# Attention's tail and the front of the first expert layer in another order, on one core

## The chip, the core and the metric

One core of a Trainium2 chip runs the whole program. Its engines work through lists of their own, in order: PE is TensorE (matmuls), DVE is VectorE, ACT is ScalarE, POOL is GpSimd, and SP issues transfers. They wait for each other by counting semaphores alone. The metric is the device time of one execution in microseconds (us); lower is better.

## What is computed

Two blocks in a row work on x, 16 sequences of 128 tokens (2048 tokens, width 256). Cut to what matters here:

```python
x = x + tanh(g_xattn[0]) * attention(layernorm(x), ctx)   # 16 heads of 16, quantised q, k, v and weights; softmax over all 2048 keys; then @ Wp + bp
x = x + tanh(g_ffn[0]) * moe(layernorm(x))                # rms norm, router to 32 experts (best 4 per token), a shared expert (704 wide) scaled by a sigmoid
x = x + tanh(g_xattn[1]) * wkv(layernorm(x), ctx)
x = x + tanh(g_ffn[1]) * moe2(layernorm(x))               # 8 experts, best 2, a shared expert
```

The change touches the end of the first line and the start of the second: the projection `@ Wp`, the norm of the new rows, the router, each token's choice of experts, and the shared expert's hidden layer.

## The kernel before, in words

**Attention.** 256 heads (16 tiles of 128 queries, 16 heads each) are worked through one after the other. A head is two units of 1024 keys (`fill_unit`, 512 units, numbered 0 to 511): two matmuls fill one of two pairs of PSUM banks, ScalarE takes the exponentials to bytes (line 485), SP transposes the head's bytes by DMA, GpSimd widens them to bf16 (the cast of line 537, into one of three buffers), and TensorE sums the values in 16 small matmuls a head (`sum_values`, line 252). A unit waits for the exponentials of the unit two before it. A cast waits until the head three before it has its values. VectorE takes maxima all along (line 426) until 701; its last tile is finished by `finish_tile`, which frees the outputs (`s_ofree`).

**The tail.** The tiles are taken in four groups of four. A group's attention outputs are turned (`turn_outputs`, line 262, 8 transposes), copied to SBUF (`copy_outputs`), and projected in two halves (`project_half`, line 270, 8 float32 matmuls each, written here as 4 instructions with two records each in the trace). VectorE adds each half to x (`add_projection`, line 369) and takes the group's statistics (`group_statistics`); ScalarE works out the deviations (`deviations`), and the group's rows are normalised: for group 0 by VectorE (`normalise`), for the others by ScalarE (`normalise_rows`, line 1358).

**The front.** Per group: the rows are turned (`turn_rows`, line 281) and copied (`copy_rows`), multiplied with the router (`router`, line 292), the logits copied (`copy_logits`), and VectorE then goes through `choose` (the four best experts; ends with `choices_marked`), `take_slots`, `weigh` (ends with `destinations_ready`, on which SP stores the rows and loads experts' weights) and `mark_slots` (a 2048-wide comparison, line 1472). TensorE counts places between them (`places`, lines 1285 and 1288) and fills a table (`fill_table`, line 1298), for which GpSimd multiplies numbers in (lines 1275 and 1276). Beside it the shared expert's hidden layer is worked out for group 0 in six columns c (`hidden0` in the code): TensorE's gate product (line 1166) and up product (line 1174), ScalarE's Silu (line 1197), VectorE's product of the two (line 1207). There is one PSUM bank for the gate and one for the up product, so that the gate of column c waits for Silu c-1, and the up product of column c for VectorE's product c-1:

```python
pe.wait_ge(sm_["gates_passed"], n)     # in shared_gate_tensor
...
pe.wait_ge(sm_["hidden_ready"], n)     # in shared_up_tensor
```

The front ends when the table is taken and the shared answers of group 0 (line 1187, 12 us of matmuls) are under way; the 32 experts follow them on TensorE.

**Order.** Nothing schedules: each engine's order is the order in which `attention_*` and `front_*` are written out by hand. Silu needs another table of ScalarE's than Ln and Exp, so each change between them loads one (`ACT_TABLE_LOAD`).

## Time and profile before

| | us |
|---|---|
| median of 3 runs | 1172.74 (1171.52 to 1173.14) |
| span of the profiled execution | 1171.5 |
| TensorE busy | 1066.6 (91%) |
| VectorE busy | 956.1 (82%) |
| ScalarE busy | 892.2 (76%) |
| GpSimd busy | 702.5 (60%) |

The profile gives the profiled execution's span and no time of its own beside it; the median lies 1.24 us above that span, and what is said of the difference between the two kernels is added to the median. All times in the stages below are us from the span's start. The attention's units end at about 724, the front reaches from there to about 778, the first group's shared answers to 791, and the experts start behind them.

### The profile page before, as it was taken

What the parts mean: (1) busy time and instruction counts of PE and PEld (TensorE: products, weight loads), DVE (VectorE), ACT (ScalarE), POOL (GpSimd) and SP (SyncE); (2) the same over time, 40 slices, a digit from 0 to 9 for tenths busy, and PEclk for the clock granted to TensorE, in tenths of its full rate; (3) what the DMA queues carried; (4) which work ended last, traced back from release to release, by engine and by line L of the source; (5) the groups of instructions that cost most, each with busy time, mean ns of one, the idle gap of its engine ahead of it and who ended that gap; (6) DMA issues with size and microseconds to landing.
All of it is one profiled execution on the core that took longest, in us unless ns stands there. A gap on an engine that the chain in (4) does not pass through costs nothing.

```text
span 1171.5 us, 24138 instructions
## 1 busy us (share of the span) xinstructions
PE 1066.6 (91%) x8396; PEld 608.8 (52%) x8396; DVE 956.1 (82%) x1748; ACT 892.2 (76%) x1546; POOL 702.5 (60%) x626
## 2 busy tenths in 40 slices
PE   8988898889988988898889988999999999999995
PEld 5743444444444444444444447756654455557774
DVE  6999999999999999999999996853328888843335
ACT  4779999999999999999999996635534567734440
POOL 3016888888787878787878785457641001543331
PEclk9999999999999999999999999799999999999998
DMA  6797987888788888888776664867937003433326
GB/s 192 121 163 146 171 171 162 171 171 173 161 171 171 173 164 173 173 169 164 155 118 110 112 109 65 244 182 213 316 98 300 1 0 85 138 102 101 102 89 222
DMA packets 388928, 176.36 MB, mean 151 GB/s; under 512 B 330542, under 2 KB 373779, under 8 KB 388809
## 3 DMA queue, kind: packets, MB, share of 16 engines
q1 hardware_dynamic: 382104, 157.85, 62.2%
q0 software_dynamic: 6480, 16.77, 4.2%
q8 instruction: 69, 1.13, 0.4%
q14 instruction: 51, 0.41, 0.1%
q10 hardware_dynamic: 224, 0.20, 0.1%
HBM read 52.70 MB, written 43.59 MB: 82 GB/s over the span
## 4 chain that ended last, share of the span: by engine, by line
PE 51%; DVE 33%; ACT 5%; issue 5%; DMA 3%; POOL 2%; SPq 1%; POOLq 0%; ACTq 0%; DVEq 0%
DVE top L426 26%; PE bank L234 10%; PE bank L220 9%; PE bank L1187 4%; PE bank L2599 4%; PE bank L252 4%; PE bank L1580 3%; PE bank L2615 3%; PE bank L1174 2%; PE bank L1166 2%; ACT weight L485 2%; PE bank L270 1%; PE bank L1598 1%; PE bank L682 1%; POOL dispatched_rows L1823 1%
## 5 line engine op out<-in xcount | busy, mean ns | idle before, releaser
L485 ACT ACTIVATE weight<-bank,bias,sq_all 128x1024 uint8<-128x1024 f32 x512 | 610.2, 1201 | 24.1 <-PE bank L234 18.9
L426 DVE TENSOR_REDUCE top<-bank 128x1 f32<-128x512 f32 (+1 forms) x683 | 610.1, 951 | 11.9 <-PE bank L220 1.6
L537 POOL CAST weight<-turned 128x2048 bf16<-128x2048 uint8 x256 | 479.4, 1895 | 44.8 <-PE bank L252 23.2
L234 PE MATMUL bank<-kT,query 128*128 128x512 bf16 x1024 | 307.7, 382 | 11.8 <-ACT weight L485 4.8
L252 PEld LDWEIGHTS bank<-v_sb,weight 128*128 128x128 bf16 x4096 | 172.0, 97 | 103.4 <-POOL weight L537 1.9
L220 PE MATMUL bank<-kT,qspace 64*128 64x512 bf16 x687 | 134.9, 386 | 55.0 <-DVE top L426 55.0
L252 PE MATMUL bank<-v_sb,weight 128*128 128x16 bf16 x4096 | 172.5, 170 | 0.6 <-POOL weight L537 0.6
L220 PE MATMUL bank<-kT,query 128*128 128x512 bf16 x337 | 127.8, 379 | 1.6 <-DVE top L426 1.4
L234 PEld LDWEIGHTS bank<-kT,query 128*128 128x128 bf16 x1024 | 59.8, 96 | 103.8 <-ACT weight L485 61.8
L1823 POOL DMA_INDIRECT dispatched_rows<-qspace,put x32 | 37.1, 1161 | 117.8 <-DVE qspace L2376 108.6
L485 ACT ACTIVATION_READ_ACCUMULATOR weight<-bank,bias,sq_all 128x1 f32 x512 | 101.3, 198 | 0.0
L220 PEld LDWEIGHTS bank<-kT,qspace 64*128 64x128 bf16 x687 | 33.3, 92 | 91.7 <-DVE top L426 86.5
L2738 POOL DMA_INDIRECT answered_rows<-yrow,target x39 | 38.0, 974 | 68.1 <-ACT yrow L2665 62.6
L2697 DVE TENSOR_TENSOR eh<-esil,bank 128x176 f32<-128x176 f32 x39 | 13.2, 338 | 60.8 <-ACT esil L2658 60.8
L520 POOL TENSOR_TENSOR shift<-shift,nsq_all 128x4 f32<-128x4 f32 (+1 forms) x65 | 13.0, 201 | 82.5 <-DVE shift L430 82.4
L220 PEld LDWEIGHTS bank<-kT,query 128*128 128x128 bf16 x337 | 32.6, 97 | 54.1 <-DVE top L426 35.4
L2599 PE MATMUL bank<-late,erowT 128*128 x156 | 52.6, 460 | 0.0
L1187 PE MATMUL bank<-sw,hT 128*128 128x256 f32 x192 | 47.5, 392 | 0.5 <-DVE source L1479 0.5
L1166 PE MATMUL bank<-xT,sw 128*128 128x512 f32 (+1 forms) x96 | 46.2, 604 | 1.6 <-ACT sil L1197 1.6
L1674 DVE TENSOR_TENSOR qspace<-wp,bank 128x176 f32<-128x176 f32 x32 | 10.8, 338 | 45.1 <-ACT wp L1631 45.1
L1174 PE MATMUL bank<-xT,sw 128*128 128x512 f32 (+1 forms) x96 | 45.8, 599 | 1.1 <-DVE hT L1207 1.1
L1713 POOL DMA_INDIRECT answered_rows<-yrow,target x32 | 31.9, 997 | 19.7 <-ACT yrow L1638 13.3
(350 smaller groups left out, 1466.2 us busy)
## 6 DMA issues: line engine op xcount, KB each, us to landing
dispatched_rows<-zeros SPq DMA_DIRECT2D x32, 524.0 KB, 3.2
...
turned<-weight SPq DMA_TRANSPOSE x256, 3.1
```

What stands on the lines that cost most here:

```text
L220: pe.matmul(bank[:, k, :], q, kT[rows, h // 2, kb * 512:(kb + 1) * 512], start=True, stop=True).then_inc(s_blk, 1)
L234: mm = pe.matmul(unit[u % 2][:, v * 512:(v + 1) * 512], query2[:, t % 2, h, :], kT[:, h // 2, first + v * 512:first + (v + 1) * 512], star ...
L252: mm = pe.matmul(bank[:, 7, h * HD:(h + 1) * HD], weight[:, m % 3, r // 2, :, r % 2], v_sb[:, r, h * HD:(h + 1) * HD], start=(r == 0), sto ...
L426: ve.tensor_reduce(top[:, first:first + count], bank[:, first % 3:first % 3 + count, :], AX.X, ALU.max).then_inc(s_max, 1)
L485: ac.activation(weight8[:, n % BYTES, u * 1024:(u + 1) * 1024], unit[u], ACT.Exp, bias=bias[:, n:n + 1], scale=sq_all[:, n:n + 1], accum_o ...
L537: po.tensor_copy(weight[:, n % 3, :, :, :].rearrange("p c q two -> p (c q two)"), turned8[:, n % 3, :, :].rearrange("p c q -> p (c q)").bi ...
L1166: mm = pe.matmul(bank[0:w, 0, :], swg[:, k, c * P:c * P + w], xT[:, k, g * 512:(g + 1) * 512], start=k == 0, stop=k == CK - 1)
L1174: mm = pe.matmul(bank[0:w, 1, :], swu[:, k, c * P:c * P + w], xT[:, k, g * 512:(g + 1) * 512], start=k == 0, stop=k == CK - 1)
L1187: mm = pe.matmul(bank[:, 6 + k % 2, 0:C], hT[0:w, c, k * P:(k + 1) * P], swd[0:w, c, :], start=c == 0, stop=c == NW0 - 1)
L1823: po.indirect_dma_start(out=dispatched1, out_offset=bass.IndirectOffsetOnAxis(ap=put1[:, t, k:k + 1], axis=0), in_=rows0[:, t, 0:ROW1], in ...
L2599: mm = pe.matmul(bank[:, 2 + b % 2, 0:2 * F1], erowT1[:, b % 2, k, :], w1gu[:, expert[b], k, :], start=k == 0, stop=k == CK - 1)
L2738: po.indirect_dma_start(out=answered1, out_offset=bass.IndirectOffsetOnAxis(ap=target1[:, b:b + 1], axis=0), in_=yrow1[:, b % YRING, :], i ...
```

## The change

Of the six half projections of groups 0 to 2, two now stand ahead of the attention's last unit and four behind it (five and one before). `finish_tile` for the last tile moves from VectorE's front to its tail, ahead of all of `choose`; group 3's outputs are turned, copied and projected ahead of the first `choose` and `places`. ScalarE's deviations of group 0 move from before the last head's exponentials to behind them. The rest of the front is in a new order on TensorE, ScalarE and VectorE. No instruction but one table load is added or taken away: ScalarE loads a table three times in the front instead of five.

```diff
--- before.py
+++ after.py
@@ -313,6 +313,10 @@
                     u = fill_unit(pe, u)
                     step = sum_values(pe, step, 9, u)
 
+                def values_to(head):
+                    nonlocal step
+                    step = sum_values(pe, step, NT * head - step, u)
+
                 unit_and_values()
                 unit_and_values()
                 pe.wait_ge(s_max, NRED)
@@ -321,35 +325,30 @@
                 unit_and_values()
                 pe.wait_ge(sm_["outputs_copied"], 1)
                 turn_outputs(pe, 1, 0)
+                unit_and_values()
+                unit_and_values()
                 project_half(pe, 0, 0, 2)
+                unit_and_values()
                 unit_and_values()
                 unit_and_values()
                 pe.wait_ge(sm_["projections_added"], 1)
                 project_half(pe, 0, 1, 2)
+                while u < NUNIT:
+                    unit_and_values()
                 pe.wait_ge(sm_["outputs_copied"], 2)
                 turn_outputs(pe, 2, 0)
-                unit_and_values()
-                unit_and_values()
+                values_to(NHEAD - 3)
                 pe.wait_ge(sm_["projections_added"], 2)
                 project_half(pe, 1, 0, 2)
-                unit_and_values()
+                values_to(NHEAD - 2)
+                pe.wait_ge(s_exp, NUNIT)
+                project_half(pe, 1, 1, 3)
+                values_to(NHEAD)
                 pe.wait_ge(sm_["projections_added"], 3)
-                project_half(pe, 1, 1, 2)
-                unit_and_values()
+                project_half(pe, 2, 0, 2)
+                turn_rows(pe, 0)
                 pe.wait_ge(sm_["projections_added"], 4)
-                project_half(pe, 2, 0, 2)
-                unit_and_values()
-                while u < NUNIT:
-                    unit_and_values()
-                project_half(pe, 2, 1, 0)
-                step = sum_values(pe, step, -step % NT, u)
-                pe.wait_ge(s_exp, NUNIT)
-                turn_rows(pe, 0)
-                step = sum_values(pe, step, NT * (NHEAD - 1) - step, u)
-                pe.wait_ge(s_wr, 32)
-                pe.wait_ge(sm_["projections_added"], 5)
-                router(pe, 0)
-                step = sum_values(pe, step, NT, u)
+                project_half(pe, 2, 1, 3)
 
             vector_steps = {"n": 0}
 
@@ -451,13 +450,16 @@
                 copy_outputs(0)
                 copy_outputs(1)
                 add_projection(ve, 0, (2, 2))
+                group_statistics(ve, 0)
                 copy_outputs(2)
-                group_statistics(ve, 0)
-                add_projection(ve, 1, (2, 2))
+                add_projection(ve, 1, (2, 3), (0,))
                 normalise(ve, 0)
-                add_projection(ve, 2, (2, 0), (0,))
+                add_projection(ve, 1, (2, 3), (1,))
                 group_statistics(ve, 1)
-                add_projection(ve, 2, (2, 0), (1,))
+                finish_tile(ve, NT - 1)
+                add_projection(ve, 2, (2, 3), (0,))
+                offsets(ve, 1)
+                add_projection(ve, 2, (2, 3), (1,))
                 group_statistics(ve, 2)
 
             def deviations(ac, g):
@@ -478,8 +480,6 @@
                         ac.wait_ge(s_turn[(n - BYTES) % 3], 16 * ((n - BYTES) // 3 + 1))
                     if h == 0 and t >= 2:
                         ac.wait_ge(s_rn, t - 1)
-                    if n == NHEAD - 1:
-                        deviations(ac, 0)
                     for u in range(2):
                         ac.wait_ge(s_unit, 2 * n + u + 1)
                         ac.activation(weight8[:, n % BYTES, u * 1024:(u + 1) * 1024], unit[u], ACT.Exp, bias=bias[:, n:n + 1],
@@ -1307,29 +1307,32 @@
                 def answers0(i):
                     shared_answers_tensor(pe, i, i)
 
+                pe.wait_ge(s_ofree, NT)
+                pe.wait_ge(sm_["outputs_copied"], 3)
+                turn_outputs(pe, 3, 0)
+                pe.wait_ge(s_wr, 32)
+                pe.wait_ge(sm_["projections_added"], 5)
+                router(pe, 0)
+                project_half(pe, 3, 0, 6)
+                project_half(pe, 3, 1, 7)
                 turn_rows(pe, 1)
+                pe.wait_ge(sm_["projections_added"], 6)
                 places(0)
-                pe.wait_ge(s_ofree, NT)
-                pe.wait_ge(sm_["projections_added"], 6)
-                turn_outputs(pe, 3, 0)
                 router(pe, 1)
                 turn_rows(pe, 2)
-                project_half(pe, 3, 0, 6)
-                project_half(pe, 3, 1, 7)
-                places(1)
-                router(pe, 2)
                 pe.wait_ge(s_wf, 64)
                 hidden0(0, 0, 1)
+                router(pe, 2)
+                places(1)
+                turn_rows(pe, 3)
+                router(pe, 3)
+                places(2)
+                hidden0(0, 1, 2)
                 fill_table(0)
-                hidden0(0, 1, 2)
-                turn_rows(pe, 3)
-                places(2)
-                router(pe, 3)
+                places(3)
                 hidden0(0, 2, 3)
-                places(3)
-                hidden0(0, 3, 4)
                 fill_table(1)
-                hidden0(0, 4, 5)
+                hidden0(0, 3, 5)
                 fill_table(2)
                 hidden0(0, 5, 6)
                 fill_table(3)
@@ -1368,41 +1371,42 @@
                         m = ac.activation(x_sb[:, t, :], x_sb[:, t, :], ACT.Identity, bias=xb[:, t:t + 1], scale=xa[:, t:t + 1])
                     m.then_inc(sm_["residuals_ready"], 1)
 
+                deviations(ac, 0)
                 ac.wait_ge(s_wn, 16)
                 copy_rows(0)
                 deviations(ac, 1)
+                copy_outputs(3)
+                normalise_rows(1)
+                copy_logits(0)
                 deviations(ac, 2)
-                copy_logits(0)
-                normalise_rows(1)
                 exponentials(0)
                 copy_rows(1)
                 normalise_rows(2)
-                copy_outputs(3)
                 copy_logits(1)
+                deviations(ac, 3)
                 copy_rows(2)
                 exponentials(1)
+                normalise_rows(3)
+                copy_logits(2)
+                shared_scalar(ac, 0, 0, 1)
+                copy_rows(3)
+                copy_logits(3)
+                shared_scalar(ac, 0, 1, 2)
                 residuals(0)
-                residuals(1)
+                ac.preload_act_table_set(LOGS)
+                exponentials(2)
+                exponentials(3)
                 ac.wait_ge(mx_["decays_bounded"], 2)
                 ac.activation(decay[:], decay[:], ACT.Exp).then_inc(mx_["decay_steps"], 1)
-                copy_logits(2)
                 ac.wait_ge(mx_["decay_steps"], 1)
                 ac.activation(decay[:], decay[:], ACT.Exp, scale=-1.0).then_inc(mx_["decay_steps"], 1)
-                deviations(ac, 3)
-                shared_scalar(ac, 0, 0, 1)
-                normalise_rows(3)
-                shared_scalar(ac, 0, 1, 2)
-                ac.preload_act_table_set(LOGS)
-                exponentials(2)
-                copy_rows(3)
-                copy_logits(3)
                 shared_scalar(ac, 0, 2, 3)
+                residuals(1)
+                shared_scalar(ac, 0, 3, 4)
                 residuals(2)
+                shared_scalar(ac, 0, 4, 5)
                 residuals(3)
-                shared_scalar(ac, 0, 3, 4)
-                ac.preload_act_table_set(LOGS)
-                exponentials(3)
-                shared_scalar(ac, 0, 4, 6)
+                shared_scalar(ac, 0, 5, 6)
 
             def front_vector(ve):
 
@@ -1484,36 +1488,31 @@
                 def answers0(i):
                     shared_answers_vector(ve, i, i)
 
-                offsets(ve, 1)
                 choose(0)
-                finish_tile(ve, NT - 1)
-                ve.wait_ge(s_ofree, NT)
                 offsets(ve, 2)
-                take_slots(0)
-                weigh(0)
-                mark_slots(0)
-                choose(1)
                 add_projection(ve, 3, (6, 7))
                 group_statistics(ve, 3)
+                choose(1)
+                offsets(ve, 3)
+                take_slots(0)
+                choose(2)
                 take_slots(1)
-                offsets(ve, 3)
+                hidden0(0, 0, 1)
+                mark_slots(0)
+                choose(3)
+                take_slots(2)
+                weigh(0)
+                mark_slots(1)
+                hidden0(0, 1, 2)
+                take_slots(3)
                 weigh(1)
-                hidden0(0, 0, 1)
-                choose(2)
-                hidden0(0, 1, 2)
-                take_slots(2)
+                mark_slots(2)
+                hidden0(0, 2, 3)
                 weigh(2)
-                choose(3)
-                hidden0(0, 2, 3)
-                take_slots(3)
-                settle()
-                mark_slots(1)
                 hidden0(0, 3, 4)
-                mark_slots(2)
+                mark_slots(3)
                 weigh(3)
-                hidden0(0, 4, 5)
-                mark_slots(3)
-                hidden0(0, 5, 6)
+                hidden0(0, 4, 6)
                 take_table()
                 answers0(0)
```

TensorE at the end of the attention, before. `L234` is a unit, `L252` are values, `L270` a half projection, `L281` turned rows, `L262` turned outputs, `L292` the router:

```order
L270 MATMUL bank<-wp,late 128x256 x4
L234 MATMUL bank<-kT,query 128x512 x2
L252 MATMUL bank<-v_sb,weight 128x16 x9
L270 MATMUL bank<-wp,late 128x256 x4
L252 MATMUL bank<-v_sb,weight 128x16 x7
L281 MATMUL bank<-ident,qspace 128x128 x8
L252 MATMUL bank<-v_sb,weight 128x16 x48
L292 MATMUL bank<-wrt,xT 128x33 x8
L252 MATMUL bank<-v_sb,weight 128x16 x16
```

The same place after; the first row is half 0,1 and the fourth the last unit:

```order
L270 MATMUL bank<-wp,late 128x256 x4
L234 MATMUL bank<-kT,query 128x512 x2
L252 MATMUL bank<-v_sb,weight 128x16 x7
L234 MATMUL bank<-kT,query 128x512 x2
L252 MATMUL bank<-v_sb,weight 128x16 x9
L262 MATMUL bank<-ident,late 128x128 x8
L252 MATMUL bank<-v_sb,weight 128x16 x23
L270 MATMUL bank<-wp,late 128x256 x4
L252 MATMUL bank<-v_sb,weight 128x16 x16
L270 MATMUL bank<-wp,late 128x256 x4
L252 MATMUL bank<-v_sb,weight 128x16 x32
L270 MATMUL bank<-wp,late 128x256 x4
```

The halves of group 1 and 2 and the turning of group 2 now stand between the values of the last five heads, no longer between the units.

TensorE in the middle of the front, after, from the shared expert's first column (`L1166`, `L1174`) to its second; `L1285` is the first row of `places`:

```order
L1166 MATMUL bank<-xT,sw 128x512 x2
L1174 MATMUL bank<-xT,sw 128x512 x2
L292 MATMUL bank<-wrt,xT 128x33 x8
L1285 MATMUL bank<-qspace,before 128x128
...
L281 MATMUL bank<-ident,qspace 128x128 x8
L292 MATMUL bank<-wrt,xT 128x33 x8
L1285 MATMUL bank<-qspace,before 128x128
...
L1166 MATMUL bank<-xT,sw 128x512 x2
L1174 MATMUL bank<-xT,sw 128x512 x2
```

Before, the first column was followed by `fill_table` (L1298) and the second column, and only then by the turned rows; now two routers, two `places` and the turned rows of group 3 stand between the two columns.

VectorE between the shared expert's first product and its second (`L1207`), before. `L1445` begins `take_slots`, `L1419` to `L1439` is `choose`:

```order
L1207 TENSOR_TENSOR hT<-sil,bank 128x512
L1419 MAX qspace<-qspace 128x8 x4
L1421 TENSOR_SCALAR qspace<-qspace 128x4
L1424 MAX_INDEX qspace<-qspace 128x8 x4
L1426 TENSOR_TENSOR qspace<-qspace 128x4x32
L1427 TENSOR_TENSOR qspace<-qspace 128x4x4
L1430 TENSOR_SCALAR qspace<-qspace 128x4x4
L1434 TENSOR_TENSOR qspace<-number,qspace 128x512
L1439 TENSOR_REDUCE qspace<-qspace 128x128
L1207 TENSOR_TENSOR hT<-sil,bank 128x512
```

The same place after, the end of it (`L1449` and `L1453` are `take_slots`, `L1458` to `L1467` `weigh`, `L1476` is `mark_slots`; ahead of these rows and behind the first product stand another `mark_slots` and a `choose`):

```order
L1449 TENSOR_TENSOR qspace<-qspace,bank 128x512
L1453 TENSOR_REDUCE qspace<-qspace 128x16
L1458 TENSOR_REDUCE qspace<-qspace 128x4
L1459 TENSOR_SCALAR sgate<-qspace 128x4
L1461 RECIPROCAL qspace<-qspace 128x4
L1462 RECIPROCAL sgate<-sgate 128x4
L1464 TENSOR_SCALAR qspace<-qspace,tgates 128x4
L1465 TENSOR_SCALAR sgate<-sgate,tgates 128x4
L1467 TENSOR_TENSOR qspace<-qspace 128x4x4
L1476 TENSOR_TENSOR late<-slot_b,qspace 128x2048
L1207 TENSOR_TENSOR hT<-sil,bank 128x512
```

Between the two products stood one `choose`; now there stand a `mark_slots`, a `choose`, a `take_slots`, a `weigh` and a second `mark_slots`.

## Rows read from the trace of the kernel before

**Rows 1.** The page's head.

```profile
span 1171.5 us, 24138 instructions
```

**Rows 2.** ScalarE in order of time: start us, us, operation, [idle before <- releaser].

```profile
709.74 1.20 ACT L485 ACTIVATE weight<-bank,bias,sq_all 128x1024 uint8<-128x1024 f32 x1 [1.66 <-PE bank L234]
...
722.74 1.20 ACT L485 ACTIVATE weight<-bank,bias,sq_all 128x1024 uint8<-128x1024 f32 x1 [1.67 <-PE bank L234]
...
729.58 2.08 ACT L1358 ACTIVATE qspace<-x_sb,nm,rec 128x256 f32<-128x256 f32 x4
```

**Rows 3.** TensorE in order of time.

```profile
722.11 0.59 PE L234 MATMUL bank<-kT,query 128*128 128x512 bf16 x2
...
731.80 1.94 PE L281 MATMUL bank<-ident,qspace 128*128 128x128 f32 x8 [2.05 <-ACT qspace L1358]
...
777.39 0.64 PE L1298 MATMUL bank<-late 128*128 128x64 bf16 x16 [0.44 <-POOL late L1276]
```

**Rows 4.** Windows: length, busy PE, PEld, DVE, ACT, POOL, then PEclk, DMA share, GB/s.

```profile
722.11:778.54 56.43, 51.54 (x364) 36.35 (x362) 49.24 (x168) 35.20 (x69) 25.30 (x27) 0.88 0.65 184
728.00:730.00 2.00, 1.75 (x29) 1.65 (x28) 1.74 (x12) 1.17 (x5) 1.23 (x2) 1.00 0.03 8
730.00:732.00 2.00, 0.20 (x1) 0.23 (x2) 1.93 (x16) 1.87 (x5) 0.00 (x0) 0.68 0.00 0
...
730.72:744.40 13.68, 12.60 (x53) 11.85 (x54) 11.84 (x42) 9.04 (x19) 7.74 (x12) 0.50 0.73 230
```

**Rows 5.** The chain that ended last, 700 to 791: start us, us, what.

```profile
714.52 1.84 PE bank L270 x8
...
735.84 3.26 PE bank L292 x16
...
746.49 1.80 PE bank L292 x16
748.29 1.80 PE bank L1166 x4
750.09 1.72 PE bank L1174 x4
...
755.78 0.88 PE bank L281 x8
...
778.54 12.01 PE bank L1187 x48
```

**Rows 6.** GpSimd in order of time.

```profile
720.04 1.90 POOL L537 CAST weight<-turned 128x2048 bf16<-128x2048 uint8 x1 [3.49 <-PE bank L252]
...
727.15 1.90 POOL L537 CAST weight<-turned 128x2048 bf16<-128x2048 uint8 x1 [0.22 <-DMA turned<-weight]
...
756.08 2.36 POOL L1275 TENSOR_SCALAR late<-qspace 128x128 bf16<-128x128 f32 x4 [9.04 <-DVE qspace L1439]
```

**Rows 7.** VectorE in order of time.

```profile
720.14 1.81 DVE L401 SCALAR_TENSOR_TENSOR nm<-mv,rec 128x8 f32<-128x8 f32 x1
...
722.26 1.38 DVE L406 TENSOR_SCALAR qspace<-x_sb,rec,nm 128x256 f32<-128x256 f32 x4
...
739.44 0.47 DVE L1419 MAX8 qspace<-qspace 128x8 f32<-128x32 f32 x4
...
741.88 1.05 DVE L1439 TENSOR_REDUCE qspace<-qspace 128x128 bf16<-128x512 f32 x1
...
764.89 0.69 DVE L1445 TENSOR_TENSOR qspace<-qspace,bank 128x512 f32<-128x512 f32 x1 [0.48 <-PE bank L1288]
...
766.33 2.29 DVE L1472 TENSOR_TENSOR late<-slot_b,qspace 128x2048 bf16<-128x2048 bf16 x1
768.54 0.68 DVE L1207 TENSOR_TENSOR hT<-sil,bank 128x512 f32<-128x512 f32 x1
769.14 2.28 DVE L1472 TENSOR_TENSOR late<-slot_b,qspace 128x2048 bf16<-128x2048 bf16 x1
771.34 0.28 DVE L1454 TENSOR_REDUCE qspace<-qspace 128x4 f32<-128x128 f32 x1
...
772.50 0.17 DVE L1463 TENSOR_TENSOR qspace<-qspace 128x16 f32<-128x16 f32 x1
```

## The prediction

> **What bounds the kernel now.** I read the page's head for the span [rows 1], then the chain of waits around the change, then each engine in order of time, and windows where the TensorE clock was not full. Up to 701 the chain is VectorE's maxima, which the change leaves alone. From about 702 on it passes to TensorE: the reader should see in [rows 2] that ScalarE, back to back until then, starts to wait for units (1.66 us before the unit of 709.74, 1.67 us before the last one of 722.74), because turned outputs and half projections stand between the units on TensorE. From the start of the last unit (722.11, [rows 3]) to the first shared answers (778.54, [rows 5]) TensorE is busy for 51.54 of 56.43 us [rows 4], so it waits for 4.9. The longest wait is 2.05 us before the turned rows of group 1 [rows 3]. The granted clock is 1.00 in 728 to 730 and 0.68 in the next 2 us, so the fall from 2.4 to 1.2 GHz is inside that wait; it stays at 0.50 to 744.4 [rows 4]. What preceded the fall was 6 us without a projection: turned rows, small values, a router of 33 columns, then the wait. In these 13.7 us TensorE was busy for 12.60 at half speed, which lost 6.3 us; a router took 3.26 us in them and 1.80 behind them [rows 5]. TensorE's work at full clock is 51.54 - 6.3 = 45.2 us. VectorE is busy for 49.24 of the same 56.43 [rows 4]: it is the near second, and that decides this case.
>
> **Step 1: the units end earlier.** Ahead of unit 511 stood two turnings and five halves counted from unit 504; now one turning and two halves. Three halves of 1.84 and a turning of 0.88 [rows 5] leave, 6.4 us. ScalarE's seven last exponentials at 1.2 us each [rows 2] could start at 708.0 to 715.1 if nothing held them; each of the two halves left still costs some 0.8, so the last starts near 716.7 instead of 722.74: 6.0 earlier. The last cast started 4.41 us after that exponential (727.15, [rows 6]), so now near 721.1, and the last head's values are summed near 723.5 instead of 729.7 (731.80 less the wait of 2.05, [rows 3]): 6.2 earlier.
>
> **Step 2: what is behind them is longer.** The same 6.4 us are done behind unit 511, which starts near 715.5. TensorE's work from there is 45.2 + 6.4 = 51.6, so with no wait and no low clock the answers would start at 767.1, 11.4 us earlier than 778.54. All now depends on the waits. TensorE fills the cast's latency with turned outputs 2 and halves 1,0 and 1,1, and waits 0.9 for the last cast. Then halves 2,0 and 2,1, turned outputs 3, router 0, halves 3,0 and 3,1 and turned rows 1 follow to 735.3 without a wait.
>
> **Step 3: the waits of the new front.** From here I placed each step behind the later of its engine and its input, with these lengths: `choose` 3.45 (739.44 to 742.93), `take_slots` 1.3 to 1.4, `mark_slots` 2.2, a product of the shared expert 0.6, `weigh` 1.33 (771.34 to 772.67) [rows 7]; group rows on ScalarE 2.0 [rows 2]; a gate 1.80 and an up product 1.72 [rows 5]. VectorE cannot begin `choose` 0 before ScalarE has turned outputs 3 copied and rows 1 normalised, since the logits' copy now stands behind both: 732.4. It then runs to 735.9; offsets, group 3's additions and statistics (behind 735.9, 3.9 us together) put `choose` 1 at 739.9 to 743.3. `normalise_rows` 3 waits for VectorE's offsets 3 at 743.9, the logits' copy of group 2 stands behind it at 746.1, and so `choose` 2 starts at 746.15. From there VectorE is full: 3.45 + 1.3 + product 0 0.6 + 2.2 + `choose` 3 3.45 + 1.3 + `weigh` 0 1.33 + 2.2 + product 1 0.6 ends at 762.6, and with `take_slots` 3, `weigh` 1, `mark_slots` 2 and product 2 (1.3 + 1.33 + 2.2 + 0.6) near 768.1.
>
> TensorE's waits against that: 0.6 for `choose` 0's marks and 0.7 for copied rows 1 (736 to 737), 0.2 and 0.6 for normalised rows 2 and 3, 2.3 before router 3 (749.2: Silu 0 and its table load now stand before `copy_rows` 3 on ScalarE), 2.4 before `places` 3 (757.9, until `take_slots` 2 has read), 2.2 before up product 2 (762.7, behind product 1), 1.5 before up product 3 (768.2, behind product 2). With the 0.9 of step 2 and small change these are 11.7 us. 767.1 + 11.7 = 778.8. The other way round, behind 768.2: up 3, gate and up 4, a table of 0.5, gate and up 5, a table make 9.7 us, and the taken table 0.8: 778.7. Before, it was 778.54. So before any lock or clock the change comes out at **+0.3**: 6.2 us won at the attention's end and 4.9 of old waits are paid back as 11.7 of new ones, and the low clock's 6.3 is paid back by the 6.4 that lay between the units.
>
> **Step 4: the port.** VectorE's small operation at 720.14 took 1.81 us and ended with GpSimd's cast of 720.04 [rows 6, 7]; so an operation with two SBUF operands can wait for GpSimd's. In the full stretch of VectorE GpSimd numbers groups 2 (from 755.7) and 3 (from 765.1), in four operations of 0.53 to 0.59 each [rows 6] and a longer one; once each, `choose` 3 or `weigh` 0 and `mark_slots` 2 can be caught. I take 0.5 each, **+1.0**; bounds 0 and 2. In 720.6 to 723 the same meeting is between the four row operations of group 0 (1.38 us, [rows 7]) and the last cast. If the cast goes first, VectorE is 1.9 late, which hides: its next deadline is the half 2,1 at 726.2. The Trainium skill, page "SBUF — State Buffer", section "SBUF: two separate sides", says that the shared pair is an exclusive lock for a whole instruction, and whoever starts first has it. By that rule the other order is possible too, with the cast up to 1.4 later; the trace agrees as far as the 1.81 us go.
>
> **Hidden edits.** Table loads on ScalarE fall from five to three; ScalarE ends no stretch after 750, so I take nothing. `destinations_ready` 0 comes near 760, behind the third `take_slots`, so SP's weights of experts 3 to 12 and the kept rows start much later than before; the last kept rows need `weigh` 3, near 774.4 against 772.67 [rows 7], and the experts read rows only at 791, behind the 12.0 us of shared answers [rows 5], which hide it. Uncovered it would cost what it is late, about 2.
>
> **The clock.** Between the first and second column of the shared expert, 743.2 to 751.5, TensorE has no wide matmul: two routers, turned rows, waits. Before, work of this kind led to the fall near 730.7 [rows 4]. So I expect a fall near 749. Router 3 then costs 1.5 more [rows 5], gate and up 1 up to 2; against it stand the waits of 2.4 and 2.2 us for VectorE that follow, and `choose` 3 needs router 3's logits only at 753.7. It hides. But the earlier stretch of 734.4 to 739.7 (turned rows, two waits, router 1) is of the same kind, if shorter. A fall there would run gate and up 0 at half speed, and router 2's logits with everything behind them would be up to 2.6 late.
>
> **Sum.** +0.3 + 1.0 = +1.3 us against the profiled execution's 1171.5 span, 1172.8. The median lies 1.24 above that span; with it **1174.0**. A difference of 0.2% (2.35 us) is about the least that a measurement tells from none.
>
> **Rivals.**
> 1. *The low clock lands on the shared products* (in 737 to 745, or twice). For it: the fall of before came 1.0 us into a wait. Against: the turned rows of 755.78, which a router followed, ran at full clock (0.88, [rows 5]), so such work does not always bring a fall. +1.3 + 2.6 = +3.9, up to +5: 1176.6 to 1178. Chance 0.27.
> 2. *TensorE, not VectorE's list, bounds the front* (the other side). If product 1 is done before gate 2 ends (760.5) and `take_slots` 2 before 755.5, the waits of 2.4, 2.2 and 1.5 go: 767.1 + 5.6 = 772.7, -5.8: 1166.9. For it: TensorE now keeps its clock over the attention's end. Against: VectorE's row of lengths above, in which only 1 us is waited. Partly true, it gives -3: 1169.7. Chance 0.17.
> 3. *The last cast loses the port* to the four row operations: the attention's end and `choose` 0 are 1.4 late, +2.7: 1175.4. By the rule of the skill's page named above this needs VectorE to start first. Chance 0.08.
> 4. *The change does nothing on balance*: clock and port both hide: +0.3, 1173.0. It goes with the forecast as to the sign; chance 0.15, and 0.33 for the forecast itself.
>
> **Chances and range.** The forecast (+1.3) and rival 4 are within 0.2%: 0.48. Rival 2 is faster: 0.17. Rivals 1 and 3 are slower: 0.35. The range goes from rival 2's partial case to rival 1's top: 1169.5 to 1177.8.
>
> **What the profile will show.** Step 1: last exponential at 716 to 717.5, last values near 723.5. Step 2: no wait of TensorE over 0.3 from 723.5 to 735. Step 3: `choose` 0 at 732 to 733, `choose` 2 at 746, VectorE full from 746 to 770, TensorE waiting for `take_slots` 2 and products 1 and 2, answers starting at 778.5 to 780.5. Step 4: single VectorE operations longer than their like by up to 0.5. The clock: below 1.00 from about 749, not before 744. Wrong if `choose` 2 starts before 744 or TensorE does not wait for products 1 and 2 (then rival 2), or if the experts wait for their rows or weights behind 791.

## The result and the profile after

The changed kernel took 1175.98 us (median of 7 runs, 1173.22 to 1178.44), the kernel before on the same chip 1172.83 (1170.89 to 1173.36, 7 runs). The ratio is 1.003, 95% interval 1.0019 to 1.0042: slower by 0.3%. In a later series of 12 runs (e12_again) it took 1174.21 against 1172.34, ratio 1.0024 (1.0013 to 1.0034). The profiled execution is the fastest of the first seven. One run of e7_list below (2528 us, mean clock 0.45) is left out of its range and ratio.

The page's head, to be held against [rows 1]:

```profile
span 1171.5 us, 24137 instructions
```

So this execution shows no loss at all. Its region starts 0.39 us earlier than in before's trace (the first turned outputs at 703.67 against 704.06); take that off before comparing. ScalarE in order of time, for [rows 2]:

```profile
716.61 1.20 ACT L485 ACTIVATE weight<-bank,bias,sq_all 128x1024 uint8<-128x1024 f32 x1
...
729.77 2.07 ACT L1361 ACTIVATE qspace<-x_sb,nm,rec 128x256 f32<-128x256 f32 x4
```

TensorE in order of time, for [rows 3] and the TensorE pieces of [rows 5]:

```profile
722.96 0.56 PE L252 MATMUL bank<-v_sb,weight 128*128 128x16 bf16 x16 [0.94 <-POOL weight L537]
...
736.30 1.97 PE L292 MATMUL bank<-wrt,xT 128*128 128x33 f32 x16 [0.34 <-ACT xT L1351]
...
739.25 1.88 PE L1166 MATMUL bank<-xT,sw 128*128 128x512 f32 x4
...
748.63 1.97 PE L292 MATMUL bank<-wrt,xT 128*128 128x33 f32 x16 [2.06 <-ACT xT L1351]
...
751.48 3.19 PE L1166 MATMUL bank<-xT,sw 128*128 128x512 f32 x4
...
757.28 0.22 PE L1285 MATMUL bank<-qspace,before 128*128 128x128 bf16 x1 [0.42 <-DVE qspace L1449]
...
762.02 1.98 PE L1174 MATMUL bank<-xT,sw 128*128 128x512 f32 x4 [1.95 <-DVE hT L1207]
...
767.29 1.98 PE L1174 MATMUL bank<-xT,sw 128*128 128x512 f32 x4 [1.02 <-DVE hT L1207]
...
777.92 12.00 PE L1187 MATMUL bank<-sw,hT 128*128 128x256 f32 x48 [0.59 <-DVE source L1483]
790.49 0.66 PE L1570 MATMUL bank<-ident,qspace 128*128 128x128 f32 x4 [0.58 <-DVE x_sb L1215]
```

The windows, with the columns of [rows 4]:

```profile
722.96:777.92 54.96, 47.20 (x305) 31.41 (x305) 48.24 (x169) 31.22 (x65) 19.24 (x25) 0.97 0.55 167
...
750.00:752.00 2.00, 2.00 (x19) 1.96 (x19) 2.00 (x3) 0.27 (x1) 0.00 (x0) 0.64 0.00 0
752.00:754.00 2.00, 2.00 (x3) 0.67 (x2) 1.97 (x11) 0.00 (x0) 0.00 (x0) 0.51 0.00 0
754.00:756.00 2.00, 2.00 (x6) 0.86 (x5) 1.93 (x10) 1.29 (x3) 0.00 (x0) 1.00 0.03 8
```

TensorE now waits for 7.8 of 55.0 us, where it waited for 4.9 of 56.4 [rows 4], and the granted clock is low (0.50, which is 1.2 GHz) for 3.4 us instead of 13.7. VectorE is busy for 48.24 of the same stretch, more than TensorE: the bound has moved. GpSimd and VectorE, for [rows 6] and [rows 7] (`choose` 0 at 732.03, `choose` 2 at 745.54):

```profile
721.01 1.90 POOL L537 CAST weight<-turned 128x2048 bf16<-128x2048 uint8 x1 [0.21 <-DMA turned<-weight]
...
764.63 4.26 POOL L1275 TENSOR_SCALAR late<-qspace 128x128 bf16<-128x128 f32 x4 [1.83 <-PE bank L1298]
```

```profile
720.99 1.94 DVE L403 TENSOR_SCALAR xb<-nm,tgates 128x4 f32<-128x4 f32 x1
...
732.03 0.47 DVE L1423 MAX8 qspace<-qspace 128x8 f32<-128x32 f32 x4 [0.60 <-ACT qspace L1356]
...
745.54 0.47 DVE L1423 MAX8 qspace<-qspace 128x8 f32<-128x32 f32 x4 [0.99 <-ACT qspace L1356]
...
764.35 2.28 DVE L1476 TENSOR_TENSOR late<-slot_b,qspace 128x2048 bf16<-128x2048 bf16 x1
```

VectorE's first `choose` and GpSimd's last group in before's trace, to be held against 732.03 and 764.63:

```profile
729.71 0.47 DVE L1419 MAX8 qspace<-qspace 128x8 f32<-128x32 f32 x4 [0.19 <-ACT qspace L1353]
```

```profile
769.55 4.13 POOL L1275 TENSOR_SCALAR late<-qspace 128x128 bf16<-128x128 f32 x4 [9.46 <-PE bank L1298]
```

### The profile page after: what moved, and what is told of

Its sections match the earlier page's. It is cut to its first block, busy times and chain, and to the rows that moved or that the text cites. A ratio compares the mean times of both kernels' runs of the same rounds, so it can differ in the third digit from the quotient of the medians.

```text
span 1171.5 us, 24137 instructions
## 1 busy us (share of the span) xinstructions
PE 1062.3 (91%) x8396; PEld 604.4 (52%) x8396; DVE 955.1 (82%) x1748; ACT 889.1 (76%) x1544; POOL 699.0 (60%) x626
## 4 chain that ended last, share of the span: by engine, by line
PE 50%; DVE 35%; ACT 5%; issue 5%; DMA 3%; POOL 2%; SPq 1%; POOLq 0%; ACTq 0%; DVEq 0%
DVE top L425 27%; PE bank L234 10%; PE bank L220 9%; PE bank L252 4%; PE bank L1187 4%; PE bank L2598 4%; PE bank L1579 3%; PE bank L2614 3%; PE bank L1174 2%; PE bank L1166 2%; ACT weight L485 2%; PE bank L1597 1%; PE bank L682 1%; POOL dispatched_rows L1822 1%; DMA late<-answered_rows 1%
## 5 line engine op out<-in xcount | busy, mean ns | idle before, releaser
L485 ACT ACTIVATE weight<-bank,bias,sq_all 128x1024 uint8<-128x1024 f32 x512 | 610.1, 1201 | 19.0 <-PE bank L234 13.7
L234 PE MATMUL bank<-kT,query 128*128 128x512 bf16 x1024 | 307.7, 382 | 12.5 <-ACT weight L485 5.3
L252 PEld LDWEIGHTS bank<-v_sb,weight 128*128 128x128 bf16 x4096 | 172.2, 97 | 103.3 <-POOL weight L537 1.0
L252 PE MATMUL bank<-v_sb,weight 128*128 128x16 bf16 x4096 | 172.5, 169 | 0.9 <-POOL weight L537 0.9
L234 PEld LDWEIGHTS bank<-kT,query 128*128 128x128 bf16 x1024 | 59.7, 96 | 104.4 <-ACT weight L485 62.9
L2737 POOL DMA_INDIRECT answered_rows<-yrow,target x39 | 38.0, 973 | 68.2 <-ACT yrow L2664 62.7
L1174 PE MATMUL bank<-xT,sw 128*128 128x512 f32 (+1 forms) x96 | 46.0, 601 | 5.0 <-DVE hT L1207 5.0
L1166 PE MATMUL bank<-xT,sw 128*128 128x512 f32 (+1 forms) x96 | 47.3, 616 | 1.5 <-ACT sil L1197 1.5
L1197 ACT ACTIVATE sil<-bank 128x512 f32<-128x512 f32 (+1 forms) x24 | 14.3, 595 | 44.6 <-PE bank L1166 34.4
```

Of the source, the lines that this page charges most:

```text
L234: mm = pe.matmul(unit[u % 2][:, v * 512:(v + 1) * 512], query2[:, t % 2, h, :], kT[:, h // 2, first + v * 512:first + (v + 1) * 512], star ...
L252: mm = pe.matmul(bank[:, 7, h * HD:(h + 1) * HD], weight[:, m % 3, r // 2, :, r % 2], v_sb[:, r, h * HD:(h + 1) * HD], start=(r == 0), sto ...
L485: ac.activation(weight8[:, n % BYTES, u * 1024:(u + 1) * 1024], unit[u], ACT.Exp, bias=bias[:, n:n + 1], scale=sq_all[:, n:n + 1], accum_o ...
L1166: mm = pe.matmul(bank[0:w, 0, :], swg[:, k, c * P:c * P + w], xT[:, k, g * 512:(g + 1) * 512], start=k == 0, stop=k == CK - 1)
L1174: mm = pe.matmul(bank[0:w, 1, :], swu[:, k, c * P:c * P + w], xT[:, k, g * 512:(g + 1) * 512], start=k == 0, stop=k == CK - 1)
L2737: po.indirect_dma_start(out=answered1, out_offset=bass.IndirectOffsetOnAxis(ap=target1[:, b:b + 1], axis=0), in_=yrow1[:, b % YRING, :], i ...
```

## The experiments

The ratio is against the runs of before on the same chip (medians 1172.3 to 1172.8). "Stage start" is TensorE's first transposes of gathered expert rows in each profile, "low" the low-clock time between 722 and 800. Before's region starts 0.4 us later in its trace than those of the others, e7_list's and e11_list_full's 0.2 to 0.3 later; so before's stage start to compare with is 790.72.

| kernel | median us (range) | ratio, 95% | stage start | low |
|---|---|---|---|---|
| before | 1172.3 to 1172.8 | | 791.11 | 13.7 |
| changed | 1175.98 (1173.2 to 1178.4) | 1.0030, 1.0019 to 1.0042 | 790.49 | 3.4 |
| e12_again (the same) | 1174.21 (1173.2 to 1177.9) | 1.0024, 1.0013 to 1.0034 | 790.87 | 6.8 |
| e1_tail | 1173.77 (1171.9 to 1177.2) | 1.0014, 1.0004 to 1.0024 | 791.61 | 10.2 |
| e2_front | 1178.57 (1177.2 to 1180.1) | 1.0054, 1.0041 to 1.0067 | 794.34 | 10.2 |
| e3_busy | 1175.12 (1174.7 to 1177.0) | 1.0024, 1.0015 to 1.0034 | 790.97 | 3.4 |
| e4_products | 1176.54 (1175.4 to 1177.8) | 1.0034, 1.0021 to 1.0047 | 789.90 | 10.2 |
| e5_weights | 1174.72 (1173.4 to 1176.6) | 1.0023, 1.0014 to 1.0031 | 793.31 | 13.7 |
| e6_both | 1173.66 (1172.1 to 1175.4) | 1.0011, 1.0002 to 1.0019 | 789.11 | 3.4 |
| e7_list | 1173.90 (1171.8 to 1175.9) | 1.0014, 1.0004 to 1.0024 | 790.14 | 6.8 |
| e8_before_busy | 1173.92 (1170.8 to 1176.1) | 1.0012, 1.0001 to 1.0023 | 790.48 | 6.8 |
| e9_before_full | 1171.93 (1171.3 to 1175.2) | 1.0004, 0.9996 to 1.0013 | 787.69 | 0 |
| e10_after_full | 1174.53 (1173.3 to 1176.3) | 1.0021, 1.0012 to 1.0031 | 790.93 | 0 |
| e11_list_full | 1176.19 (1173.4 to 1179.9) | 1.0033, 1.0020 to 1.0047 | 792.31 | 6.8 |

### The two halves of the change: e1_tail, e2_front

e1_tail is the kernel before with the changed attention's end alone (router 0 behind the last projections); e2_front is the kernel before up to the last unit, with the changed lists of the front. The cut of e1_tail:

```diff
+                while u < NUNIT:
+                    unit_and_values()
                 pe.wait_ge(sm_["outputs_copied"], 2)
                 turn_outputs(pe, 2, 0)
...
+                project_half(pe, 2, 1, 3)
                 pe.wait_ge(s_wr, 32)
                 pe.wait_ge(sm_["projections_added"], 5)
                 router(pe, 0)
```

> The attention's tail of the changed kernel (four halves behind the last unit, last tile finished in it) with the front's three lists of the kernel before; router 0 stays ahead of the front. Theory A (the front's lists decide, step by step as in the prediction, and the low clock comes on top): the tail's waits are gone but 6.4 us of TensorE work lie behind the units, the old wait of 2.05 us and its low clock come back a little later: +2.6 us against before (range +1.5 to +4). Theory B (the longer tail alone is what costs, the new front is free or a gain): the whole of the changed kernel's +3.1 or more is here, and e2_front is at or below before. Last exponential 6 us earlier than before under both.

> The attention's tail of the kernel before with the front's lists of the changed kernel (turned outputs 3 first, choose 0 behind them). Theory A: the attention ends as late as before, choose 0 waits for turned outputs 3 and normalised rows 1 behind it, and the VectorE chain from choose 2 to product 2 is as long as in the changed kernel: +6 us against before (range +4 to +8). Theory B: at or below before (0 to -3). So the two parts would each be slower alone than together under A.

The tail alone costs 0.14% (+1.2 us, below the range of theory A), the front alone 0.54% (+6.0, as expected). The front's lists are the dearer half and need the earlier end of the attention that the tail gives them: in e2_front the answers start at 781.77. The tail alone ends its units 6 us earlier, and nothing of it is left at the answers (779.04 against before's 778.54, or 778.15 less the later start of its trace). TensorE of e1_tail shows where it went:

```profile
734.78 1.94 PE L281 MATMUL bank<-ident,qspace 128*128 128x128 f32 x8 [4.10 <-ACT qspace L1361]
```

Before's wait of 2.05 us for normalised rows 1 [rows 3] is 4.10 here, and the clock falls inside it as before.

### TensorE kept busy in some of the changed kernel's waits: e3_busy

```diff
+                pe.wait_ge(sm_["outputs_copied"], 4)
+                busy(3, 0)
                 places(0)
+                busy(1, 0)
                 router(pe, 1)
...
                 places(1)
+                pe.wait_ge(sm_["projections_added"], 2 * NG)
+                busy(2, 6)
                 turn_rows(pe, 3)
+                busy(8, 6)
                 router(pe, 3)
```

`busy(n, b)` is n products of 512 columns into a bank that nobody reads.

> The changed kernel plus 14 matmuls of 512 bf16 columns of ones on TensorE whose results nobody reads: 3 into bank 0 before the first places, 1 before router 1, 2 before turned rows 3 and 8 before router 3, all where TensorE waits anyway (0.7, 0.3, 0.6 and 2.1 us in the trace after). They take 0.22 us each. Theory A with the clock as the rest of the loss: the granted clock stays at 1.00 up to 1160, the runs lie within 1.5 us of each other instead of 5, and the median falls to the changed kernel's fastest run: 1173.2 +- 0.6, +0.4 against before, -2.7 against the changed kernel. If the clock has no part in it: +3.1 as the changed kernel, with the same spread.

The spread went from 5.2 to 2.3 us, and no run was above 1177.0. The median stayed at 1175.12, 1.9 above what I expected. The clock fell once more, now at 757.8, after a wait of 2.07 us before `places` 3. That the runs with the highest times are gone goes with theory A; that the median did not reach 1173.2 goes against it.

### Late kept rows: e4_products, e5_weights, e6_both

e4_products moves VectorE's products 1 to 3 ahead; e5_weights issues all owned experts' weights before the first kept rows; e6_both has both, and `weigh` 3 ahead of the last marks.

```diff
-                for e in range(3):
+                for e in range(OWN):
                     load_expert(sp, e)
...
-                    for e in range(3 + 2 * g, min(5 + 2 * g, OWN)):
-                        load_expert(sp, e)
```

> The changed kernel, VectorE's list in the front alone altered: product 1 directly behind take_slots 2 (before weigh 0 and mark_slots 1), product 2 directly behind take_slots 3, product 3 before weigh 2. Theory A (products 1 and 2 late on VectorE hold the up products): the wait of 1.95 us before up product 2 and of 1.02 before up product 3 shrink, end of the front 1.5 us earlier in a run of equal clock; -1.3 us against the changed kernel, so +1.8 against before (range 0 to +3). Rival C (late weights and rows of the experts, not VectorE, set the start of the experts): no change, +3.1; in the trace TensorE would then wait for rows or weights behind 791, which the trace after does not show.

> The changed kernel with one edit in SyncE's list: the loads of all ten owned experts' weights are issued before the first kept rows, instead of two behind each of the four kept-row stores. The four stores then stand alone behind their waits. Theory R (the late kept rows and the weights queued behind them are what the new front gives back between its end and the second expert layer): some 1 to 2 us less than the changed kernel, 1174 to 1175, and the wait of GpSimd's first gather for kept rows shrinks from 9.9 us to about 5. Theory F (all of the loss lies in the front's own order and TensorE's clock): no difference to the changed kernel, 1176 +- 0.8, ratio to before 1.003. I lean to F for this kernel, since in its trace TensorE waited for no row in the experts' stage (78.59 us, as before's 78.58).

> The earlier products on VectorE of run e4_products together with the loads of run e5_weights, and the last weights of the router (weigh 3) ahead of the last marks. In e4_products the front's answers began 1.1 us earlier than in the changed kernel, but the last kept rows landed late, the first gather came at 785.42, and the experts' stage took 81.22 us instead of 78.59. Theory R: the stage is back at 78.6, 2.6 us less than e4_products: 1173.9 (1173 to 1175). Theory F (the longer stage had another cause): 1176.5 as e4_products, and the stage stays above 80 us.

GpSimd's first gather of kept rows in e4_products, and then in e6_both:

```profile
785.42 1.26 POOL L1551 DMA_INDIRECT qspace<-kept_rows,source  x1 [15.56 <-DMA kept_rows<-qspace]
```

```profile
777.48 1.26 POOL L1549 DMA_INDIRECT qspace<-kept_rows,source  x1 [8.37 <-DVE source L1481]
```

In e4_products the last kept rows are issued at 778.9 (775.0 in the changed kernel), the gather waits for the kept rows' landing, and the experts' stage took 81.22 us instead of 78.59. In e6_both the last of them goes out near 770.5, the gather waits only for its index list, and the stage is back at 78.58. The median is 2.9 us lower, as theory R had it (1173.66, expected 1173.9), but not by this alone: e6_both's answers also start 0.7 us earlier (776.53 against 777.27), and its stage behind the experts is 1.5 us longer (182.19 against 180.64). Which of its two edits brought the stage back, the early loads or `weigh` 3, is not separated. Its products come in time, and the answers start 1.4 us earlier than in the changed kernel (777.92), so about that much was the price of the late products. e5_weights alone lies between the two series of the changed kernel (1174.72), and no difference is shown. There is some cover for the late rows: in e3_busy the first gather comes at 782.25, 8.7 us ahead of the stage (10.0 in the changed kernel), and the stage still took 78.59.

The profile of e5_weights, however, caught what the changed kernel's does not. Its TensorE list is the same. TensorE in order of time, and the windows:

```profile
736.27 2.51 PE L292 MATMUL bank<-wrt,xT 128*128 128x33 f32 x16 [0.33 <-ACT xT L1349]
738.60 1.95 PE L281 MATMUL bank<-ident,qspace 128*128 128x128 f32 x8
740.34 3.62 PE L1166 MATMUL bank<-xT,sw 128*128 128x512 f32 x4
...
793.31 0.66 PE L1568 MATMUL bank<-ident,qspace 128*128 128x128 f32 x4 [0.58 <-DVE x_sb L1215]
```

```profile
736.00:738.00 2.00, 1.73 (x14) 1.73 (x14) 1.97 (x6) 2.00 (x5) 1.82 (x5) 0.88 1.15 306
738.00:744.00 6.00, 6.00 (x17) 3.93 (x18) 5.79 (x30) 3.36 (x10) 2.52 (x3) 0.50 1.16 310
```

Up to router 1 the two executions agree within 0.03 us. Then the clock falls during router 1 here (low from 737.5 to 744.4) and not in the other (there it stays full to 750); the first gate product takes 3.62 instead of 1.88, router 3 comes 2.4 us later (751.06), a second fall of the same length follows from 751.2, and the stage starts 2.8 us later.

e5_weights issues other transfers from 737.3 on, and these could be thought the reason. e4_products settles it: no engine's list differs from the changed kernel's before 749, its transfers are the changed kernel's, and it fell during router 1 too:

```profile
736.29 2.33 PE L292 MATMUL bank<-wrt,xT 128*128 128x33 f32 x16 [0.33 <-ACT xT L1351]
...
740.17 2.37 PE L1166 MATMUL bank<-xT,sw 128*128 128x512 f32 x4
...
749.38 1.97 PE L292 MATMUL bank<-wrt,xT 128*128 128x33 f32 x16 [2.13 <-ACT xT L1351]
```

```profile
736.00:738.00 2.00, 1.71 (x14) 1.71 (x15) 1.97 (x6) 2.00 (x5) 1.83 (x5) 0.93 1.15 306
738.00:740.00 2.00, 2.00 (x11) 2.00 (x12) 1.93 (x15) 0.99 (x5) 1.46 (x1) 0.50 1.10 299
```

Its early stretch was half as long (3.4 us against 6.8), and router 3 came only 0.75 us late (749.38 against 748.63).

### A front in which TensorE finds its inputs: e7_list, e11_list_full

e7_list has the changed tail, the loads of e5_weights and new lists. TensorE's steps around router 1:

```diff
-places 0, router 1, rows 2, gate 0, up 0, router 2, places 1, rows 3, router 3, places 2, gate 1, up 1, table 0
+router 1, gate 0, places 0, rows 2, gate 1, up 0, router 2, places 1, rows 3, up 1, table 0, router 3, gate 2, gate 3, up 2
```

e11_list_full adds eight fillers before rows 3 and nine before gate 3.

> The changed kernel's attention, so all four half projections still behind the last unit, but the front's three lists (TensorE, ScalarE, VectorE) in an order in which TensorE is meant to find its inputs ready: shared gate and up products stand between routers 1, 2 and 3, the places come later, and the router's weights come early. With the durations of the changed kernel's rows and full clock, TensorE's answers end 5.6 us earlier than in the changed kernel. Theory T (the front can be bound by TensorE's own work, and then the time comes out at the end): 1170 to 1171.5, ratio to before 0.998 to 0.999, no low clock in the front, TensorE's idle time between 722 and the answers under 3 us instead of 8. Rival V (VectorE's and ScalarE's shared resources stretch their lists as soon as they are full, or a later stage takes the gain back): 1173 or more, no better than before.

> The kernel of e7_list with eight fillers ahead of the transposes of group 3's rows (there it waited 2.12 us, and the clock was low from 746.9 to 754.3) and nine ahead of the fourth gate product (1.82 us). Theory T2 (the low clock is what kept this list from its 5.6 us): the experts' stage starts at 786.5 (785.8 to 787.8) instead of 790.14, median 1169.5 (1168.5 to 1171), ratio to before 0.997, so faster than both kernels. Rival: ScalarE's and VectorE's lists are late by what TensorE gains, and the stage starts at 789 or later, median 1172 or more.

TensorE of e7_list in order of time:

```profile
749.08 1.94 PE L281 MATMUL bank<-ident,qspace 128*128 128x128 f32 x8 [2.12 <-ACT qspace L1366]
750.82 3.62 PE L1174 MATMUL bank<-xT,sw 128*128 128x512 f32 x4
...
777.56 12.00 PE L1187 MATMUL bank<-sw,hT 128*128 128x256 f32 x48 [0.50 <-DVE source L1489]
```

The list gave 0.4 to 0.6 us at the answers (777.56 against 777.92, with a trace that starts 0.2 later; I had worked out 5.6): the clock fell at 747.7, inside a wait of 2.12 us for ScalarE's rows, and stayed low to 754.5, and VectorE, busy for 50.6 of the 56 us from 722 to 778, has hardly any more to give. The fillers of e11_list_full kept the clock in that wait, and then TensorE waited 1.87 us before router 3 and the clock was low from 754.2 to 761; gate 2 took 3.76. That theory (T and T2) fell; neither version beats the kernel before.

### What the low clock is worth to each order: e8_before_busy, e9_before_full, e10_after_full, e12_again

e9_before_full (e8_before_busy has only the first of the three):

```diff
+                busy(8, 6)
                 turn_rows(pe, 1)
                 places(0)
...
                 project_half(pe, 3, 1, 7)
+                busy(6, 0)
                 places(1)
...
                 places(2)
+                busy(3, 6)
                 router(pe, 3)
```

e10_after_full is e3_busy with eight, six and four more ahead of `places` 3, up 2 and up 3.

> The kernel before with eight filler products (1.7 us at full clock) on TensorE in its wait of 2.05 us for the normalised rows (ahead of the transposes of group 1's rows); everything else is as before. Theory C (before's stretch at low clock, 730.7 to 744.4, lies on the path): the stretch stays at full clock, its 12.6 us of busy time shrink to 6.3, VectorE's choices come earlier, and the kernel ends some 4 us earlier, 1168.6 (1167.5 to 1170), ratio 0.9965. Theory H (the low clock hid behind VectorE's and GpSimd's work, as I priced the fall in the changed kernel): within 1 us of before, 1172.6. In between would say that the clock falls again at the next wait.

> The kernel before with fillers in three of TensorE's waits: eight products ahead of the transposes of group 1's rows (as in e8_before_busy), six ahead of places 1 (there e8_before_busy waited 1.67 us, after which its clock fell on the shared products), three ahead of router 3. Theory D (the two orders differ by 4 us at full clock, and before's low clock gives most of that away): the clock stays full to the answers, places 1 at 742.5, and the experts' stage starts 3.5 to 4.5 us ahead of before's 791.11, at 787.0 (786.6 to 787.6); median 1169 (1168 to 1170.5). Theory H (the order at full clock is worth nothing, other waits take the place of the low clock): stage from 790.5 or later, median 1172 to 1174.

> The changed kernel with the fillers of e3_busy and, besides, eight products ahead of places 3 (where e3_busy waited 2.07 us and then lost 3.4 us to low clock), six ahead of the third up product and four ahead of the fourth. Theory D: the clock stays full to the answers, but VectorE's list is what TensorE waits for in the second half, so nothing more is won than the low clock cost: the experts' stage starts at 790.4 (790.0 to 791.0), as in the changed kernel's fastest run, the spread of the runs is under 3 us, and the median is 1173.2 to 1174.5. With e9_before_full at 787.0 the two orders then differ by 3.4 us at full clock. Theory K (the clock alone is what makes the changed kernel slow): the stage starts at 787 to 788, median 1170 to 1171.

> The changed kernel once more, unchanged, beside the others: 1176 (median of 12 runs between 1175 and 1176.8), runs from 1173 to 1178.5; in its profile the front's low clock is 3.4 us when the experts' stage starts at 790.5, and some 10 to 14 us, with a stretch from 736 on over router 1 and the first shared products, when the stage starts at 793. If the stage's start does not go with the low clock, my account of the changed kernel's spread is wrong.

TensorE of e8_before_busy:

```profile
742.46 0.23 PE L1285 MATMUL bank<-qspace,before 128*128 128x128 bf16 x1 [1.67 <-DVE qspace L1444]
...
744.64 3.59 PE L1166 MATMUL bank<-xT,sw 128*128 128x512 f32 x4
...
758.03 3.33 PE L1166 MATMUL bank<-xT,sw 128*128 128x512 f32 x4
```

With the long low stretch gone, `places` 1 came at 742.46 instead of 745.96, which is 3.1 us earlier after the 0.4 of the traces' starts. But behind the next wait, 1.67 us for VectorE, the clock fell onto the first gate product, a second fall followed at 758.5, and 0.2 us was left (790.48 against 790.72). The median, 1173.92, is no better than before's; theory C had 1168.6. e9_before_full filled those too. Its TensorE, and its window from 722 to 778:

```profile
740.68 1.46 PE L1312 MATMUL bank<-every 128*128 128x512 bf16 x6
742.51 0.23 PE L1285 MATMUL bank<-qspace,before 128*128 128x128 bf16 x1 [0.38 <-DVE qspace L1446]
...
744.69 1.96 PE L1166 MATMUL bank<-xT,sw 128*128 128x512 f32 x4
...
787.69 0.66 PE L1578 MATMUL bank<-ident,qspace 128*128 128x128 f32 x4 [0.58 <-DVE x_sb L1215]
```

```profile
722.00:778.00 56.00, 52.42 (x391) 34.17 (x389) 48.24 (x167) 35.28 (x69) 26.93 (x29) 1.00 0.69 196
```

and e10_after_full in the same two views:

```profile
759.89 1.46 PE L1312 MATMUL bank<-every 128*128 128x512 bf16 x6
762.46 1.98 PE L1174 MATMUL bank<-xT,sw 128*128 128x512 f32 x4 [1.11 <-DVE hT L1207]
...
790.93 0.66 PE L1586 MATMUL bank<-ident,qspace 128*128 128x128 f32 x4 [0.58 <-DVE x_sb L1215]
```

```profile
722.00:778.00 56.00, 52.46 (x337) 33.17 (x336) 49.36 (x169) 31.20 (x65) 18.39 (x26) 1.00 0.53 156
```

This is the reading that the study turns on. At full clock throughout, the old order starts the stage at 787.69 and the new one at 790.93: the change costs 3.24 us, as theory D had it (3.4). The new order's second half goes at VectorE's pace: even with fillers TensorE waits another 1.11 us for product 1. The median of e10_after_full is 2.6 us above that of e9_before_full.

The full clock also moved GpSimd. With gate 1 at full speed the table comes earlier, GpSimd's numbering of group 2 starts at 755.34 instead of 757.02, and its long operation runs beside VectorE's `weigh` 0. The same line of `weigh` in e12_again (no GpSimd work beside it), in the changed kernel, and in e10_after_full:

```profile
758.41 0.23 DVE L1464 TENSOR_SCALAR qspace<-qspace,tgates 128x4 f32<-128x4 f32 x1
```

```profile
758.49 0.30 DVE L1464 TENSOR_SCALAR qspace<-qspace,tgates 128x4 f32<-128x4 f32 x1
```

```profile
758.80 0.57 DVE L1480 TENSOR_SCALAR qspace<-qspace,tgates 128x4 f32<-128x4 f32 x1
```

From the start of `weigh` 0 to `mark_slots` 1 the three take 1.17, 1.32 and 1.76 us. `mark_slots` 1 starts 0.43 later in e10_after_full than in the changed kernel (759.52 against 759.09), and the same distance stands at up 2 (762.46, 762.02) and at the stage's start (790.93, 790.49). So up to 0.6 of the 3.24 us are this meeting, and the fall that e10_after_full does not have had hidden.

e12_again was to show that the stage's start goes with the low clock. Its median, 1174.21, is below the expected 1175 to 1176.8, and its profile drew neither of the two cases: one fall at 749.6, low for 6.8 us, stage at 790.87. Together with the changed kernel, e3_busy and e10_after_full it says that up to 6.8 us of low clock behind 749 leave the stage between 790.49 and 790.97: they hide.

Only 0.4 of e9_before_full's gain of 3.1 us in the front (791.11 less 0.37, its earlier start, against 787.69) reached its median, which theory D had at 1169. One reason is that the fillers did not hold the clock in every run: five of the twelve have a mean clock of 0.991 or 0.992, against 0.996 in the profiled one. But the four runs with 0.996 have a median of 1171.6, only 0.7 below before's. In the profile most of the gain went in the stage behind the experts: 181.64 us against 179.68. SyncE's eight issues of the fetches of answered rows, in e9_before_full and then in e7_list:

```profile
871.81 5.34 SPq L1782 DMA_DIRECT2D late<-answered_rows  x8
```

```profile
874.25 3.87 SPq L1783 DMA_DIRECT2D late<-answered_rows  x8
```

These issues took 3.7 to 6.1 us over all profiles, and the longest landing 9.0 to 10.6, although the code is the same there. Whether an earlier front makes them longer, I could not tell from one profile of each; e6_both's stage was 182.19 us long with issues of 3.74 and a clock fall near 890, so they are not the only way in which the stage gets longer.

## Why the prediction was half right

**The change's own arithmetic (steps 1 to 3).** Right. The last exponential started at 716.61 (716.7 predicted), the last values were done at 723.5 (723.5), TensorE had no wait from there to 734.9, `choose` 0 began at 732.03 (732.4), `choose` 2 at 745.54 (746.15), product 1 was done at 762.0 (762.6), and the waits stood where they were forecast: 2.06 before router 3 (2.3), 1.95 before up 2 (2.2), 1.02 before up 3 (1.5). The 2.4 before `places` 3 were 0.42, since a low-clock gate 1 filled 1.3 of them and `take_slots` 2 was done 0.7 earlier than worked out. The answers started at 777.92 plus 0.39, 778.3 against 778.8 predicted: -0.2 against before, where +0.3 was forecast.

**Step 4, the port, +1.0.** The mechanism is right, the term was too large as a difference between the kernels. `weigh` 0 was caught, as named: by 0.15 us in the changed kernel's profile and by 0.6 in e10_after_full's (above). Where VectorE's 2.28 us operation started first, GpSimd became longer: its four operations from 764.63, behind VectorE's of 764.35, took 4.26 us instead of 2.36 [rows 6], and VectorE's kept its length. But the kernel before had such meetings as well, and the prediction charged them to the changed one alone: its last group took 4.13 (769.55), the long operation behind it 3.56 instead of 1.56, and TensorE's last table waited 0.44 us for it [rows 3], a wait that is gone now. The meeting at 720.99 happened (1.94 us for a small operation, until the cast was done) and hid, as said. The Trainium skill, page "SBUF — State Buffer", section "SBUF: two separate sides", says that the shared pair is an exclusive lock for a whole instruction, and whoever starts first has it. The trace agrees at 764.63; at 720.99 VectorE is recorded 0.02 us ahead of the cast and waited all the same, so to that precision the starts do not tell the winner.

**Hidden edits.** The late kept rows hid, as forecast, and had at least 1.3 us to spare (e3_busy). A last store 3.9 us later, in e4_products, cost 2.6 us in the experts' stage. The prediction's "about 2" was for a smaller delay; the mechanism was right.

**The clock.** This is the step that failed. I expected one fall near 749, which hides, and gave the fall in 737 to 745 a chance of 0.27 as rival 1, worth 2.6 us. The fall near 750 came and hid: e10_after_full, with none at all, starts the stage no earlier (790.93 against 790.49). But the early fall is not an alternative to it: e4_products and e5_weights had both, with the changed kernel's lists up to there, and it made router 3 late by 0.75 and 2.4 us. The prediction gave one forecast and one rival; the kernel draws among falls that differ in place, number and length from run to run.

Of the 19 runs of the changed kernel the 11 with a mean granted clock of 0.993 and more lie between 1173.2 and 1175.2, median 1173.7; the 8 with 0.992 and less lie between 1175.8 and 1178.4, median 1176.7. Against before as a whole (1172.5) they are 1.2 and 4.2 above, near my +1.3 and rival 1's +3.9. That nearness is in part luck, for before draws too: of its 33 runs in the last series the 17 with 0.991 and more have a median of 1171.8, the 16 with 0.990 and less one of 1173.0. Faster group against faster group the change costs 1.9 us, slower against slower 3.7. That the second group of the changed kernel are executions with the early fall is not shown: no profile of the unchanged kernel fell into it, and the mean clock also counts the low stretch at each execution's end (7.9 to 11.4 us in the profiles). It fits e5_weights (mean 0.990) and e4_products (0.992), and e10_after_full, whose fillers leave no run with a clock under 0.994 and none above 1176.3.

The 6.3 us that the prediction charged to before's low clock are TensorE's lost busy time. With fillers in its waits, before's stage starts only 3.1 us earlier.

**The sum.** I took before's profiled execution as base and put the median 1.24 above its span. In the series here a run's time is 1.7 above its span, so that execution stands for 1173.2, above the median of before, and the changed kernel's is the fastest of its seven. Two equal spans of 1171.5 hide a difference of 1.9 to 3.2 us of the medians. The sum of +1.3 missed that by 0.6 to 1.9 us. If the slower group of runs is the early fall, it raises the mean by 1.3 us (8 of 19 runs, 3.0 each); but before's slower group raises its mean by 0.7 (16 of 33, 1.5 each), so the net is 0.6. The stage between the experts and the second layer took 180.4 to 180.6 in the profiles of the changed kernel and e5_weights, 179.7 in before's. Why, stays open, and so does the rest.

**Rival 2, TensorE bounds the front,** fell: TensorE waited for products 1 and 2 as the prediction had them, and e7_list, an order made for it, still began the answers at 777.56. **Rival 3** did not occur: the cast at 721.01 went first.

**Why the change does not help.** It removes a low clock that cost before 3.1 us, and puts VectorE's list in its place, which costs 3.2 at full clock; the new order then draws its own falls, early or late. The 6.2 us won at the attention's end are real and are spent before 733, since VectorE's first choice waits for ScalarE's copied and normalised rows: it starts at 732.03, where before's starts at 729.71. In the profiled executions the two fronts end level (790.49 and 790.87 against 790.72).
